# One batch's output tiles drained by ScalarE instead of VectorE, with x added between DRAM tensors, in a fused mixing and routed low-rank kernel

## The chip, the cores and the metric

One core of a Trainium2 chip runs the whole program. The metric is the device time of one execution in microseconds (us), as the median over several runs. All arithmetic is in 32-bit floats; the matrix products split each operand into a high and a low float32r part and use three products of the four.

## What is computed

Four batches of 1024 tokens with 1024 channels. Per channel and batch a bidirectional decaying sum over tokens mixes the side input f with itself, is gated by a sigmoid of x, and goes through a linear layer with a routed low-rank addition; the input x is added at the end.

```python
ek, ekv = exp(min(f, 30)), exp(min(f, 30)) * f
num = fwd_scan(ekv) + bwd_scan(ekv) - ekv + exp(min(u + f, 30)) * f      # state * decay + next
den = fwd_scan(ek)  + bwd_scan(ek)  - ek  + exp(min(u + f, 30))
y = sigmoid(x) * num / max(den, 1e-8) * (0.8 + 0.2 * tf)                 # 4 x 1024 x 1024
h = silu(y @ rw1.T + rb1)                                                # router, 64 wide
logits = h @ rw2.T + rb2 + gates                                         # 16 experts, top 2
coeff = softmax of the top two, 0 elsewhere
out = x + y @ W.T + bias + sum over experts of (coeff * (y @ A_e.T)) @ B_e.T
```

## The kernel before, in words

Everything lies channel-major: 128 channels on the partitions, tokens along the free dimension. A **unit** is one block of 128 channels of one batch with all 1024 tokens; there are 32, eight (CB) per batch. A **group** G is half the tokens (512) of one batch, so there are eight groups; groups 0 and 1 are the first batch. An output tile e = 8 G + j is 128 output channels j by 512 tokens.

Each engine has a program of its own, one loop over 41 **steps** s, and semaphores tie them. In step s:

- VectorE (loop at L856) runs for unit s the forward scans of the denominator (L704) and the numerator (L708), the `ratio` of unit s - 1 (L747), the backward scan of the denominator (L713), `p2` (L718), `sum_den` (L723), `scale_e` of unit s + 1 (L692) and the backward scan of the numerator (L734).
- ScalarE (L493) does `scale_end_den` (L414), `scale_end_num` (L414), `split_hi` (y_hi, L402), `exp_uk` (L391), `exp_k` (L385), `sigmoid_r` (L426), a table load (L478), and `inverse` (L430, L432), in that order.
- GpSimd (L638) does `sum_n` (L580) and `gate_n` (L586) of unit s - 1, `split_lo` (y_lo, L612), and `p1` of unit s + 1 (L602). The forward scan of step s + 1 waits for that p1.
- SyncE issues the loads of f (`load_k`, L294) and x (`load_r`, L299) for the next units, the weights, and the loads of x tiles for the output.

TensorE takes the finished y tiles: for a group `hid` (router), `low_rank`, `base` (the linear layer), `logits`, `spread` (routing weights onto partitions) and `expert`. Groups 0 and 1 get the lower half of the linear layer's sum as soon as half the channels are there: 16 part tiles, which ScalarE copies to the buffer `xo` (`drain_part`, L476) and SyncE stores into `out`. The upper half with the experts comes later. For these first 16 tiles VectorE runs `evacuate` (L754): PSUM tile plus bias plus an x tile that SyncE had loaded into the same `xo` buffer, written to `xo`; then GpSimd issues `add_out` (L636), a DMA that adds the tile onto what is stored in `out`. `xo` has six buffers (tile e uses e % 6). The units of the second batch are 8 to 15; group 2 is its late half of tokens, and TensorE takes unit 14, then 15, last. Unit 15 is handled in two halves (`HALVED`).

The order of the extra work of the first batch (steps CB to CB + 6, that is 8 to 14) is written out by hand in tables keyed by step and by place within the step: `hidden_at`, `silu_at`, `routing_at`, `weigh_at`, `evacs_at` for VectorE (places AFTER_FWD and so on, L163), `adds_at` for GpSimd (AFTER_GATE: after gate_n; AFTER_LO: after split_lo), `x_loads_at` for SyncE. The routing of group 1 lies in step CB + 4 = 12 after the forward scan of the denominator, its `weigh` (L818) after the ratio; the routing of group 0 lies in step 9 after the backward scan of the denominator, its weigh after p2. After routing, ScalarE makes wx_hi (L470) and GpSimd wx_lo (L625), both needed by `expert`; in steps 9 and 12 GpSimd does wx_lo ahead of p1.

From group 2 on (`SPLIT`) nothing is added by DMA: VectorE evacuates with bias and x, and SyncE stores. In the reader's listing:

Of the kernel before, what the change touches and what calls it, by code (L numbers as in the profile page):

```python
# [7 lines left out]
def decay_mix_with_routed_lora_channel_major(nc, x_cm, f_cm, cond, w, u, w_router_a, w_base, w_expert, bias, rb1, rw2,  # L8
# [25 lines left out]
    with ExitStack() as ctx:  # L34
# [6 lines left out]
        def sem(name):  # L41
            return ctx.enter_context(nc.semaphore(name))
# [117 lines left out]
        def base_from(G):  # L160
# [4 lines left out]
        silu_at = {(CB + 1, AFTER_FWD): 0, (CB + 3, AFTER_BWD_NUM): 1}  # L165
        routing_at = {(CB + 1, AFTER_BWD_DEN): 0, (CB + 4, AFTER_FWD): 1}
        weigh_at = {(CB + 1, AFTER_P2): 0, (CB + 4, AFTER_RATIO): 1}
        evacs_at = {(CB + 2, AFTER_FWD): (0, 1), (CB + 2, AFTER_FWD_NUM): (1, 2), (CB + 2, AFTER_RATIO): (2, 3),
                    (CB + 2, AFTER_SUM): (3, 5), (CB + 2, AFTER_BWD_NUM): (5, 6), (CB + 3, AFTER_FWD_NUM): (6, 7),
                    (CB + 3, AFTER_RATIO): (7, 8), (CB + 4, AFTER_BWD_NUM): (8, 10), (CB + 5, AFTER_FWD): (10, 11),  # L170
                    (CB + 5, AFTER_FWD_NUM): (11, 12), (CB + 5, AFTER_RATIO): (12, 13), (CB + 5, AFTER_SUM): (13, 14),
                    (CB + 5, AFTER_BWD_NUM): (14, 15), (CB + 6, AFTER_FWD): (15, 16)}
        AFTER_GATE, AFTER_LO = range(2)
        adds_at = {(CB + 2, AFTER_LO): (0, 3), (CB + 3, AFTER_GATE): (3, 6), (CB + 4, AFTER_GATE): (6, 8),
                   (CB + 5, AFTER_GATE): (8, 10), (CB + 5, AFTER_LO): (10, 13), (CB + 6, AFTER_GATE): (13, 16)}
        AFTER_K, AFTER_R = range(2)
        x_loads_at = {(CB, AFTER_R): (2, 6), (CB + 1, AFTER_R): (0, 2), (CB + 2, AFTER_R): (6, 9),
                      (CB + 3, AFTER_R): (9, 12), (CB + 4, AFTER_R): (12, 14), (CB + 5, AFTER_K): (14, 16),
                      (CB + 6, AFTER_K): (16, 19), (CB + 6, AFTER_R): (19, 20)}

        def tiles(table, s, place):
            return range(*table.get((s, place), (0, 0)))
# [13 lines left out]
        def held(g):  # L196
            return g >= 2 * CB and g % CB in (1, 5)

        def stores_to(slot, end):
            return sum(1 for e in range(PARTS, end) if e % XBUF == slot)  # L200
# [77 lines left out]
        def _(sp):  # L278
# [59 lines left out]
            for s in range(STEPS):  # L338
# [27 lines left out]
                for n in chunks_at(load_late_steps, s):  # L366
                    load_chunk(n)
                if s == CB:
                    for i in range(PBUF):
                        sp.wait_ge(part_stored[i], 16 * (PARTS // PBUF))  # L370
                if s == CB + 1:
                    sp.wait_ge(w_lo_ready, CHUNKS)
                for e in tiles(x_loads_at, s, AFTER_R):
                    load_x(e)
            for i in range(XBUF):
                sp.wait_ge(out_added[i], 16 * len(range(i, PARTS, XBUF)))
                sp.wait_ge(out_stored[i], 16 * stores_to(i, GROUPS * CB))

        @block.scalar
        def _(act):  # L380
# [91 lines left out]
            def drain_part(p):  # L472
# [20 lines left out]
            for s in range(STEPS):  # L493
# [7 lines left out]
                if s < UNITS:  # L501
                    if s == 0:
                        act.wait_ge(recip_ready, 1)
                    scale_end_den(s)
                if q == 1:
                    exp_gap(G)
                if s == CB + 1:
                    copy_xa(0)
                if s == CB + 4:
                    exp_gap(1)  # L510
                    copy_xa(1)
                if s < UNITS:
                    if s - 1 in HALVED:
                        split_late_hi(s - 1)
                    scale_end_num(s)
                if 0 < s <= UNITS and not late_split:
                    split_hi(s - 1)
                if q == 1:
                    split_wx(G)
                if s < UNITS:  # L520
                    exp_uk(s)
                if s == CB + 4:
                    split_wx(1)
                if s + 1 < UNITS:
                    exp_k(s + 1)
                if s == CB + 1:
                    exp_gap(0)
# [7 lines left out]
                if s < UNITS:  # L535
                    sigmoid_r(s)
                if z_of == 0:
                    low_rows(z_of)
                if z_of >= 0:
                    sigmoid_z(z_of)  # L540
                if s < UNITS or z_of >= 0:
                    exps()
                if s == CB + 1:
                    split_wx(0)
                if s < UNITS:
                    if s == 0:
                        act.wait_ge(gains_ready, 2)
                    inverse(s)
                for n in new:
                    weights_hi(n)  # L550
# [7 lines left out]
        def _(pool):  # L558
# [74 lines left out]
            def add_out(e):  # L633
                pool.wait_ge(evacuated, e + 1)
                pool.wait_ge(part_stored[e % PBUF], 16 * (e // PBUF + 1))
                nc.gpsimd.dma_start(at(out, e), xo[:, e % XBUF, :], accum_op=ALU.add).then_inc(out_added[e % XBUF], 16)  # L636

            for s in range(STEPS):  # L638
# [7 lines left out]
                if s - 1 in HALVED:  # L646
                    split_late_lo(s - 1)
                    split_lo(s - 1)
                for e in tiles(adds_at, s, AFTER_GATE):
                    add_out(e)  # L650
# [4 lines left out]
                if 0 < s <= UNITS and not late_split and s - 1 not in HALVED:  # L655
                    split_lo(s - 1)
                for e in tiles(adds_at, s, AFTER_LO):
                    add_out(e)
# [13 lines left out]
        def _(dve):  # L672
# [77 lines left out]
            def evacuate(G, j):  # L750
                e, bank = G * CB + j, out_bank(G, j)
                dve.wait_ge(out_done, e + 1)
                dve.wait_ge(x_in[e % XBUF], 16 * (e // XBUF + 1))
                nc.vector.scalar_tensor_tensor(out=xo[:, e % XBUF, :], in0=acc[:, bank, :], scalar=bias_sb[:, j:j + 1],  # L754
                                               in1=xo[:, e % XBUF, :], op0=ALU.add, op1=ALU.add).then_inc(evacuated, 1)
# [88 lines left out]
            def first_groups(s, place):  # L844
                if (s, place) in hidden_at:
                    hidden(hidden_at[s, place])
                if (s, place) in silu_at:
                    silu(silu_at[s, place])
                if (s, place) in routing_at:
                    routing(routing_at[s, place])  # L850
                if (s, place) in weigh_at:
                    weigh(weigh_at[s, place])
                for e in tiles(evacs_at, s, place):
                    evacuate(*divmod(e, CB))

# [288 lines left out]
```

## Time and profile before

| what | value |
|---|---|
| median of 3 runs | 688.63 us (688.4 to 689.16) |
| profiled execution, its own time | 688.6 us |
| its span in the profile | 686.6 us |
| TensorE busy | 598.7 us (87%) |
| VectorE busy | 526.6 us (77%) |
| GpSimd busy | 368.1 us (54%) |
| ScalarE busy | 357.1 us (52%) |
| DMA queue of SyncE | 73.79 MB |
| DMA queue of GpSimd | 4.20 MB |

The names in the profile: PE is TensorE (matmul), PEld its weight loads, DVE is VectorE, ACT is ScalarE, POOL is GpSimd, SPq is SyncE's DMA queue. A row names the line of the kernel, the tile written and the tiles read. In brackets at its end stands how long the engine was idle before it and whose work ended that. Times are in us from the start of the span unless ns is said. Busy shares over the whole span hide that the stages differ: VectorE is over 90% busy up to some 310 us, TensorE from some 260 us to the end.

### The profile page before, as it was taken

Reading aid. Unit: us, or ns where it says so; the run is one execution under the profiler, and the core shown is the slowest. Engines: PE = TensorE matmul, PEld = TensorE weight load, DVE = VectorE, ACT = ScalarE, POOL = GpSimd, SP = SyncE. Lnnn points to the kernel's source line nnn. Section 1 sums busy time; section 2 is a strip of 40 time slices with the busy share of each in tenths; the row PEclk is TensorE's granted clock in tenths of the full one; section 3 lists DMA queues with packets and bytes.
Section 4 is the critical chain, followed back from the end, with each engine's and each line's share of the span. In section 5 each row is a group of like instructions: output and inputs, shape, how many; then the busy total and the mean of one; then the engine's idle time right before and its main releaser. Section 6 shows DMA issues by size and latency. Waiting matters only on the chain.

```text
span 686.6 us, 7030 instructions
## 1 busy us (share of the span) xinstructions
PE 598.7 (87%) x2626; PEld 490.1 (71%) x2626; DVE 526.6 (77%) x573; ACT 357.1 (52%) x418; POOL 368.1 (54%) x183
## 2 busy tenths in 40 slices
PE   0153588989999937999999999999999999999997
PEld 0132466768878825887888878888888888888886
DVE  7999999999999999998899797979897532021202
ACT  4777789785656666655655554656465420011000
POOL 1789997867868876647544753565465501000100
PEclk9976799989999978999999999999999999999999
DMA  5323476522945831234423360427132402040022
GB/s 190 122 90 121 124 254 205 194 100 71 215 107 121 203 113 64 74 113 160 141 73 113 109 198 32 153 63 242 33 116 84 124 29 66 27 153 1 25 67 76
DMA packets 33169, 78.42 MB, mean 114 GB/s; under 512 B 4720, under 2 KB 4848, under 8 KB 33136
## 3 DMA queue, kind: packets, MB, share of 16 engines
q1 hardware_dynamic: 30832, 73.79, 33.2%
q0 software_dynamic: 2304, 4.20, 3.8%
q8 instruction: 20, 0.33, 0.2%
q14 instruction: 13, 0.11, 0.0%
HBM read 57.00 MB, written 20.97 MB: 114 GB/s over the span
## 4 chain that ended last, share of the span: by engine, by line
PE 49%; DVE 25%; POOL 16%; issue 7%; ACT 1%; DMA 1%; SPq 0%; DVEq 0%; POOLq 0%; ACTq 0%
PE acc L925 15%; PE acc L927 15%; PE acc L926 15%; DVE mix L713 5%; POOL mix L602 4%; POOL kv L580 4%; POOL yr L586 4%; DVE yr L747 3%; DVE mix L708 3%; DVE eu L723 3%; DVE kv L718 2%; DVE xo L754 2%; POOL y_lo L612 2%; DVE mix L734 2%; PE acc L936 1%
## 5 line engine op out<-in xcount | busy, mean ns | idle before, releaser
L925 PE MATMUL acc<-y_hi,wa_hi 128*128 128x512 f32 x640 | 258.5, 404 | 59.7 <-POOL y_lo L612 52.7
L926 PE MATMUL acc<-y_lo,wa_hi 128*128 128x512 f32 x640 | 255.3, 399 | 0.0
L927 PE MATMUL acc<-y_hi,wa_lo 128*128 128x512 f32 x640 | 254.8, 398 | 0.0
L925 PEld LDWEIGHTS acc<-y_hi,wa_hi 128*128 128x128 f32 x640 | 124.1, 194 | 89.3 <-POOL y_lo L612 54.1
L927 PEld LDWEIGHTS acc<-y_hi,wa_lo 128*128 128x128 f32 x640 | 123.8, 194 | 26.7
L926 PEld LDWEIGHTS acc<-y_lo,wa_hi 128*128 128x128 f32 x640 | 124.2, 194 | 25.6
L602 POOL TENSOR_TENSOR mix<-mix,kv 128x1024 f32<-128x1024 f32 x31 | 74.3, 2397 | 75.7 <-DVE mix L692 59.4
L754 DVE SCALAR_TENSOR_TENSOR xo<-acc,bias_sb,xo 128x512 f32<-128x512 f32 x64 | 46.4, 735 | 75.2 <-PE acc L927 75.2
L612 POOL TENSOR_TENSOR y_lo<-yr,y_hi 128x1024 fp32r<-128x1024 f32 x31 | 74.3, 2398 | 50.2 <-ACT y_hi L402 50.2
L625 POOL TENSOR_TENSOR wx_lo<-xa,wx_hi 128x512 fp32r<-128x512 f32 x16 | 20.9, 1329 | 129.3 <-ACT wx_hi L470 129.3
L580 POOL TENSOR_TENSOR kv<-mix,kv 128x1024 f32<-128x1024 f32 (+1 forms) x32 | 75.4, 2356 | 5.3 <-DVE mix L734 5.3
L704 DVE TENSOR_TENSOR_SCAN mix<-d_ps,mix 128x1024 f32<-128x1024 f32 x32 | 73.1, 2284 | 5.8 <-POOL mix L602 5.7
L414 ACT ACTIVATE mix<-mix,rdelta_g 128x1 f32<-128x1 f32 x64 | 18.6, 296 | 111.6 <-DVE mix L708 71.6
L586 POOL TENSOR_TENSOR yr<-kv,yr 128x1024 f32<-128x1024 f32 (+1 forms) x32 | 75.2, 2351 | 2.5
L713 DVE TENSOR_TENSOR_SCAN mix<-d_ps,mix 128x1023 f32<-128x1023 f32 x32 | 74.8, 2336 | 0.3 <-ACT mix L414 0.3
L734 DVE TENSOR_TENSOR_SCAN mix<-d_ps,mix 128x1023 f32<-128x1023 f32 (+1 forms) x32 | 73.7, 2303 | 0.0
L708 DVE TENSOR_TENSOR_SCAN mix<-d_ps,mix 128x1024 f32<-128x1024 f32 x32 | 72.7, 2272 | 0.0
L402 ACT ACTIVATE y_hi<-yr 128x1024 fp32r<-128x1024 f32 x31 | 32.9, 1060 | 51.6 <-DVE yr L747 51.6
L747 DVE SCALAR_TENSOR_TENSOR yr<-eu,limit_g,yr 128x1024 f32<-128x1024 f32 (+1 forms) x32 | 40.2, 1257 | 22.5 <-POOL yr L586 22.5
L925 PE MATMUL acc<-wx_hi,wb_hi 128*128 128x512 f32 x128 | 50.0, 391 | 1.8 <-POOL wx_lo L625 1.8
L926 PE MATMUL acc<-wx_lo,wb_hi 128*128 128x512 f32 x128 | 49.8, 389 | 0.0
L927 PE MATMUL acc<-wx_hi,wb_lo 128*128 128x512 f32 x128 | 49.8, 389 | 0.0
(98 smaller groups left out, 738.3 us busy)
## 6 DMA issues: line engine op xcount, KB each, us to landing
kv<-f_cm SPq DMA_DIRECT2D x32, 512.0 KB, 3.6
yr<-x_cm SPq DMA_DIRECT2D x32, 512.0 KB, 3.4
out<-xo SPq DMA_DIRECT2D x64, 256.0 KB, 4.2
xo<-x_cm SPq DMA_DIRECT2D x64, 256.0 KB, 3.9
out<-xo POOLq DMA_DIRECT2D x16, 256.0 KB, 6.8
xa<-w_base SPq DMA_DIRECT2D x5, 512.0 KB, 3.5
xo<-w_base SPq DMA_DIRECT2D x3, 512.0 KB, 5.7
xo<-w_router_a SPq DMA_DIRECT2D x2, 480.0 KB, 3.6
```

Of the source, the lines that this page charges most:

```text
L580: nc.gpsimd.tensor_tensor(kv[:, g % 2, t], num_of(g)[:, t], kv[:, g % 2, t], ALU.add).then_inc(n_ready, 1)
L586: nc.gpsimd.tensor_tensor(yr[:, g % 2, t], kv[:, g % 2, t], yr[:, g % 2, t], ALU.mult).then_inc(gated, 1)
L602: nc.gpsimd.tensor_tensor(num_of(g), den_of(g), kv[:, g % 2, :], ALU.mult).then_inc(p1_ready, 1)
L612: nc.gpsimd.tensor_tensor(slots(y_lo, g), yr[:, g % 2, :].rearrange("p (h t) -> p h t", h=2), slots(y_hi, g).bitcast(fp32), ALU.subtract). ...
L704: nc.vector.tensor_tensor_scan(den_of(g), decay(g, T), den_of(g), 0.0, ALU.mult, ALU.add).then_inc(den_fwd, 1)
L708: nc.vector.tensor_tensor_scan(num_of(g), decay(g, T), num_of(g), 0.0, ALU.mult, ALU.add).then_inc(num_fwd, 1)
L713: nc.vector.tensor_tensor_scan(rev(den_of(g)), decay(g, T - 1), rev(den_of(g)), den_of(g)[:, T - 1:T], ALU.mult, ALU.add).then_inc(den_bwd, 1)
L734: nc.vector.tensor_tensor_scan(a[:, stop - 1::-1], decay(g, stop), a[:, stop - 1::-1], a[:, stop:stop + 1], ALU.mult, ALU.add).then_inc(nu ...
L747: nc.vector.scalar_tensor_tensor(out=yr[:, g % 2, t], in0=eu[:, t], scalar=limit_f[:, g:g + 1], in1=yr[:, g % 2, t], op0=ALU.min, op1=ALU. ...
L925: nc.tensor.matmul(out_ap, wh, yh, start=start, stop=False)
L926: nc.tensor.matmul(out_ap, wh, yl, start=False, stop=False)
L927: return nc.tensor.matmul(out_ap, wl, yh, start=False, stop=stop)
```

## The change

The 16 output tiles of groups 0 and 1 are no longer evacuated by VectorE. ScalarE does it (`drain`: activation Identity with the bias), in places of its own program set by a new table, `drains_at`. x isn't loaded for them any more; GpSimd issues eight DMAs (`add_x`) that add a whole unit of x (128 rows of 1024 floats, both token halves) from DRAM onto `out` in DRAM, after the part tiles are stored there, and `add_out` of a tile waits for the x add of its channels. A drain of tile e from the seventh on waits until the output add of tile e - 6 has landed, because it writes the same `xo` buffer. The routing of group 1 moves within step 12 from after the forward scan to after the backward scan of the denominator, and its weigh from after the ratio to after sum_den. On ScalarE the copy of xa and the exponential of the gap for group 1 move behind exp_uk, and the split of wx behind the table load. Of SyncE's x loads, those for tiles 0 to 15 go, and 16 to 19 move.

```diff
-        routing_at = {(CB + 1, AFTER_BWD_DEN): 0, (CB + 4, AFTER_FWD): 1}
-        weigh_at = {(CB + 1, AFTER_P2): 0, (CB + 4, AFTER_RATIO): 1}
-        evacs_at = {(CB + 2, AFTER_FWD): (0, 1), (CB + 2, AFTER_FWD_NUM): (1, 2), (CB + 2, AFTER_RATIO): (2, 3),
-                    (CB + 2, AFTER_SUM): (3, 5), (CB + 2, AFTER_BWD_NUM): (5, 6), (CB + 3, AFTER_FWD_NUM): (6, 7),
-                    (CB + 3, AFTER_RATIO): (7, 8), (CB + 4, AFTER_BWD_NUM): (8, 10), (CB + 5, AFTER_FWD): (10, 11),
-                    (CB + 5, AFTER_FWD_NUM): (11, 12), (CB + 5, AFTER_RATIO): (12, 13), (CB + 5, AFTER_SUM): (13, 14),
-                    (CB + 5, AFTER_BWD_NUM): (14, 15), (CB + 6, AFTER_FWD): (15, 16)}
+        routing_at = {(CB + 1, AFTER_BWD_DEN): 0, (CB + 4, AFTER_BWD_DEN): 1}
+        weigh_at = {(CB + 1, AFTER_P2): 0, (CB + 4, AFTER_SUM): 1}
+        AFTER_END_DEN, AFTER_END_NUM, AFTER_EXP_UK, AFTER_EXP_K, AFTER_SIGMOID, AFTER_INVERSE = range(6)
+        drains_at = {(CB + 1, AFTER_INVERSE): (0, 1), (CB + 2, AFTER_END_DEN): (1, 3), (CB + 2, AFTER_EXP_UK): (3, 4),
+                     (CB + 2, AFTER_SIGMOID): (4, 5), (CB + 2, AFTER_INVERSE): (5, 6), (CB + 3, AFTER_END_DEN): (6, 7),
+                     (CB + 3, AFTER_EXP_UK): (7, 8), (CB + 4, AFTER_INVERSE): (8, 9), (CB + 5, AFTER_END_DEN): (9, 11),
+                     (CB + 5, AFTER_EXP_UK): (11, 12), (CB + 5, AFTER_SIGMOID): (12, 13),
+                     (CB + 5, AFTER_INVERSE): (13, 14), (CB + 6, AFTER_END_DEN): (14, 15),
+                     (CB + 6, AFTER_EXP_UK): (15, 16)}
         AFTER_GATE, AFTER_LO = range(2)
-        adds_at = {(CB + 2, AFTER_LO): (0, 3), (CB + 3, AFTER_GATE): (3, 6), (CB + 4, AFTER_GATE): (6, 8),
-                   (CB + 5, AFTER_GATE): (8, 10), (CB + 5, AFTER_LO): (10, 13), (CB + 6, AFTER_GATE): (13, 16)}
+        x_adds_at = {(CB, AFTER_LO): (0, 1), (CB + 1, AFTER_GATE): (1, 3), (CB + 1, AFTER_LO): (3, 4),
+                     (CB + 2, AFTER_GATE): (4, 8)}
+        adds_at = {(CB + 2, AFTER_LO): (0, 2), (CB + 3, AFTER_GATE): (2, 5), (CB + 3, AFTER_LO): (5, 7),
+                   (CB + 4, AFTER_GATE): (7, 8), (CB + 5, AFTER_LO): (8, 11), (CB + 6, AFTER_GATE): (11, 13),
+                   (CB + 6, AFTER_LO): (13, 15), (CB + 7, AFTER_GATE): (15, 16)}
-        x_loads_at = {(CB, AFTER_R): (2, 6), (CB + 1, AFTER_R): (0, 2), (CB + 2, AFTER_R): (6, 9),
-                      (CB + 3, AFTER_R): (9, 12), (CB + 4, AFTER_R): (12, 14), (CB + 5, AFTER_K): (14, 16),
-                      (CB + 6, AFTER_K): (16, 19), (CB + 6, AFTER_R): (19, 20)}
+        x_loads_at = {(CB + 6, AFTER_R): (16, 18), (CB + 7, AFTER_R): (18, 20)}
...
+            def drain(e):
+                G, j = divmod(e, CB)
+                act.wait_ge(out_done, e + 1)
+                if e < 2:
+                    act.wait_ge(w_lo_ready, CHUNKS)
+                elif e < XBUF:
+                    act.wait_ge(part_stored[(e - 2) % PBUF], 16 * (PARTS // PBUF))
+                else:
+                    act.wait_ge(out_added[e % XBUF], 16 * (e // XBUF))
+                nc.scalar.activation(xo[:, e % XBUF, :], acc[:, out_bank(G, j), :], ACT.Identity,
+                                     bias=bias_sb[:, j:j + 1]).then_inc(evacuated, 1)
...
+                drains(s, AFTER_END_DEN)
                 if q == 1:
                     exp_gap(G)
                 if s == CB + 1:
                     copy_xa(0)
-                if s == CB + 4:
-                    exp_gap(1)
-                    copy_xa(1)
...
                     exp_uk(s)
+                drains(s, AFTER_EXP_UK)
                 if s == CB + 4:
-                    split_wx(1)
+                    copy_xa(1)
+                    exp_gap(1)
...
-                if s == CB + 1:
-                    split_wx(0)
+                if s in (CB + 1, CB + 4):
+                    split_wx((s - CB) // 4)
...
             def add_out(e):
                 pool.wait_ge(evacuated, e + 1)
-                pool.wait_ge(part_stored[e % PBUF], 16 * (e // PBUF + 1))
+                pool.wait_ge(x_added[e % CB], 16)
                 nc.gpsimd.dma_start(at(out, e), xo[:, e % XBUF, :], accum_op=ALU.add).then_inc(out_added[e % XBUF], 16)
+
+            def add_x(j):
+                pool.wait_ge(part_stored[j % PBUF], 16 * ((j + CB) // PBUF + 1))
+                nc.gpsimd.dma_start(out[j], x_cm[j], accum_op=ALU.add, max_dma_last_dim=4 * T).then_inc(x_added[j], 16)
...
-                for e in tiles(evacs_at, s, place):
-                    evacuate(*divmod(e, CB))
```

The other drains stand after `scale_end_num`, `exp_k`, `sigmoid_r` and `inverse` (places without an entry in the table do nothing).

## Rows read from the trace of the kernel before

**Rows 1.** Waits, TensorE, 150 to 400 us: who waited, for whom, us, times, longest.
```profile
PE acc L936 <- POOL y_lo L612: 8.9, 1, 8.9
PE acc L936 <- POOL y_lo L619: 5.4, 1, 5.4
```

**Rows 2.** Busy time by stretch; at the end granted clock, DMA share, GB/s.
```profile
240.00:260.00 20.00, 6.25 (x17) 4.12 (x15) 19.00 (x14) 12.28 (x15) 15.49 (x10) 0.71 0.30 101
```

**Rows 3.** Timeline of VectorE, the forward scans that open steps 9 to 15.
```profile
136.41 2.27 DVE L704 TENSOR_TENSOR_SCAN mix<-d_ps,mix 128x1024 f32<-128x1024 f32 x1
...
157.09 2.29 DVE L704 TENSOR_TENSOR_SCAN mix<-d_ps,mix 128x1024 f32<-128x1024 f32 x1 [1.27 <-POOL mix L602]
...
174.01 2.27 DVE L704 TENSOR_TENSOR_SCAN mix<-d_ps,mix 128x1024 f32<-128x1024 f32 x1
...
189.54 2.27 DVE L704 TENSOR_TENSOR_SCAN mix<-d_ps,mix 128x1024 f32<-128x1024 f32 x1
...
210.20 2.27 DVE L704 TENSOR_TENSOR_SCAN mix<-d_ps,mix 128x1024 f32<-128x1024 f32 x1
...
226.45 2.27 DVE L704 TENSOR_TENSOR_SCAN mix<-d_ps,mix 128x1024 f32<-128x1024 f32 x1
...
240.42 2.29 DVE L704 TENSOR_TENSOR_SCAN mix<-d_ps,mix 128x1024 f32<-128x1024 f32 x1 [0.26 <-POOL mix L602]
```

**Rows 4.** The chain of waits around step 15: start, us, what.
```profile
237.98 2.24 POOL mix L602
240.33 2.38 POOL kv L580
242.78 2.35 POOL yr L586
245.23 1.28 DVE yr L747
...
251.76 1.17 POOL mix L602
```

**Rows 5.** Groups of instructions, VectorE, 156 to 232 us.
```profile
L754 DVE SCALAR_TENSOR_TENSOR xo<-acc,bias_sb,xo 128x512 f32<-128x512 f32 x16 | 11.5, 728 | 0.0
```

**Rows 6.** Timeline of GpSimd in step 10.
```profile
159.49 2.40 POOL L586 TENSOR_TENSOR yr<-kv,yr 128x1024 f32<-128x1024 f32 x1
165.23 2.42 POOL L612 TENSOR_TENSOR y_lo<-yr,y_hi 128x1024 fp32r<-128x1024 f32 x1 [3.34 <-ACT y_hi L402]
167.58 2.80 POOL L636 DMA_DIRECT2D out<-xo  x3
171.28 2.40 POOL L602 TENSOR_TENSOR mix<-mix,kv 128x1024 f32<-128x1024 f32 x1 [0.90 <-DVE mix L692]
```

**Rows 7.** Groups of instructions, ScalarE, 100 to 260 us.
```profile
L391 ACT ACTIVATE eu<-kv,u_g 128x1024 f32<-128x1024 f32 x10 | 11.0, 1102 | 0.0
...
L402 ACT ACTIVATE y_hi<-yr 128x1024 fp32r<-128x1024 f32 x10 | 10.6, 1061 | 11.3 <-DVE yr L747 11.3
...
L476 ACT COPY xo<-acc 128x512 f32<-128x512 f32 x9 | 4.7, 583 | 0.0
```

**Rows 8.** Timeline of SyncE's queue, x loads behind the first output adds.
```profile
173.83 0.33 SPq L312 DMA_DIRECT2D xo<-x_cm  x1
...
176.41 0.33 SPq L312 DMA_DIRECT2D xo<-x_cm  x1
```

**Rows 9.** DMA queues, whole span: packets, MB, share of 16 engines.
```profile
q1 hardware_dynamic: 30832, 73.79, 33.2%
q0 software_dynamic: 2304, 4.20, 3.8%
```

**Rows 10.** Timeline of VectorE, the first weighing of step 9.
```profile
150.18 0.69 DVE L818 TENSOR_TENSOR xa<-acc,xa 128x512 f32<-128x512 f32 x1
```

**Rows 11.** Timeline of TensorE, behind a wait for the router.
```profile
139.41 1.86 PE L974 MATMUL acc<-rw_sb,fan 64*128 64x16 f32 x8 [2.45 <-DVE fan L764]
...
141.78 0.63 PE L926 MATMUL acc<-y_lo,wa_hi 128*128 128x512 f32 x1
```

More of the change, by code:

```diff
@@ L197, in held, with x_loads_to @@
             return g >= 2 * CB and g % CB in (1, 5)
+        def x_loads_to(e):
+            return sum(1 for i in range(PARTS, e + 1) if i % XBUF == e % XBUF)
         def stores_to(slot, end):
@@ L213, in decay_mix_with_routed_lora_channel_major @@
         part_out = sem("part_out")
+        x_added = [sem(f"x_added{j}") for j in range(CB)]
         out_added = [sem(f"out_added{i}") for i in range(XBUF)]
@@ L367, in _ @@
                     load_chunk(n)
-                if s == CB:
-                    for i in range(PBUF):
-                        sp.wait_ge(part_stored[i], 16 * (PARTS // PBUF))
-                if s == CB + 1:
-                    sp.wait_ge(w_lo_ready, CHUNKS)
                 for e in tiles(x_loads_at, s, AFTER_R):
                     load_x(e)
+            for j in range(CB):
+                sp.wait_ge(x_added[j], 16)
             for i in range(XBUF):
@@ L476, in drain_part, with drains @@
                 nc.scalar.copy(xo[:, 2 + p % PBUF, :], acc[:, p % 5, :]).then_inc(part_out, 1)
+            def drain(e):
[9 more added lines that the diff above has]
+                                     bias=bias_sb[:, j:j + 1]).then_inc(evacuated, 1)
+            def drains(s, place):
+                for e in tiles(drains_at, s, place):
+                    drain(e)
             exps = lambda: nc.scalar.preload_act_table_set("natural_log_exp_and_others")
@@ L515, in _ @@
                     scale_end_num(s)
+                drains(s, AFTER_END_NUM)
                 if 0 < s <= UNITS and not late_split:
@@ L521, in _ @@
                     exp_uk(s)
+                drains(s, AFTER_EXP_UK)
                 if s == CB + 4:
-                    split_wx(1)
+                    copy_xa(1)
+                    exp_gap(1)
                 if s + 1 < UNITS:
                     exp_k(s + 1)
+                drains(s, AFTER_EXP_K)
                 if s == CB + 1:
@@ L536, in _ @@
                     sigmoid_r(s)
+                drains(s, AFTER_SIGMOID)
                 if z_of == 0:
@@ L542, in _ @@
                     exps()
-                if s == CB + 1:
-                    split_wx(0)
+                if s in (CB + 1, CB + 4):
+                    split_wx((s - CB) // 4)
                 if s < UNITS:
@@ L548, in _ @@
                     inverse(s)
+                drains(s, AFTER_INVERSE)
                 for n in new:
@@ L648, in _ @@
                     split_lo(s - 1)
+                for j in tiles(x_adds_at, s, AFTER_GATE):
+                    add_x(j)
                 for e in tiles(adds_at, s, AFTER_GATE):
@@ L656, in _ @@
                     split_lo(s - 1)
+                for j in tiles(x_adds_at, s, AFTER_LO):
+                    add_x(j)
                 for e in tiles(adds_at, s, AFTER_LO):
@@ L752, in evacuate @@
                 dve.wait_ge(out_done, e + 1)
-                dve.wait_ge(x_in[e % XBUF], 16 * (e // XBUF + 1))
+                dve.wait_ge(x_in[e % XBUF], 16 * x_loads_to(e))
                 nc.vector.scalar_tensor_tensor(out=xo[:, e % XBUF, :], in0=acc[:, bank, :], scalar=bias_sb[:, j:j + 1],
```

## The prediction

> **What bounds the kernel now.** I first read who waited for whom on TensorE. From 150 us on it has two long waits, 8.9 us and 5.4 us, both for a y_lo tile of GpSimd [rows 1]. The stretch 240 to 260 us is the only later one with a hole: TensorE is busy 6.25 of 20 us there, at a granted clock of 0.71 [rows 2]. Both waits are for the last two channel tiles (units 14 and 15) of the second batch; the late half of unit 15 lets TensorE go at 260.55. Behind that TensorE is all but full to the end. So the question is one number: how much earlier does unit 15 come? A microsecond won there is a microsecond of the kernel; one won anywhere else is nothing.
>
> What sets unit 15 is the loop of steps on VectorE. Its step starts are the forward scans [rows 3]: steps 9 to 15 start at 136.41, 157.09, 174.01, 189.54, 210.20, 226.45 and 240.42. They took 20.7, 16.9, 15.5, 20.7, 16.25 and 14.0 us (9 to 14). The chain of waits shows a step without extras as a cycle through two engines: p1, sum_n and gate_n on GpSimd, then the ratio and three more passes on VectorE, and p1 again [rows 4], 251.76 - 237.98 = 13.8 us. No step falls below 13.8 us by taking evacuations from VectorE alone.
>
> **What is removed.** 16 evacuations, 11.5 us of VectorE, 0.728 each [rows 5]. They start some 0.65 us apart from their neighbours, so they are worth at most 16 x 0.65 = 10.4 us, by steps 6, 2, 2, 5 and 1 of them (10 to 14). Against the floor of the cycle much of it is not to be had. The 16 x loads leave SyncE's queue; nothing that decides waits for them, so I cost that at nothing.
>
> **What is added.** On GpSimd, eight more DMA issues. Three in a row took 2.80 us there, 0.93 each [rows 6]. A DRAM to DRAM issue has no row; between nothing and twice 0.93, I take 0.93, since it moves the same number of 128 rows. On ScalarE 16 drains; the nearest row is the copy of the same shape, 0.583 [rows 7]. I take 0.6. On the DMA queue of GpSimd, 8 accumulations of 512 KB.
>
> **Step 10.** gate_n ends where its row does, 161.9 [rows 6]. Then come four x adds (to 165.6), y_lo 2.4 (168.0), two output adds (169.9), p1 2.4 (172.3). VectorE without its evacuations would be ready at 170.7, so GpSimd decides: step 11 starts at 172.4 instead of 174.0, a gain of 1.6. Drains 1 to 5 fall into idle time of ScalarE.
>
> **Step 11, the place that decides.** The drain of tile 6 stands after scale_end_den, ahead of scale_end_num, split_hi and exp_uk, and it waits until the output add of tile 0 has landed, because both use buffer 0. Before, only an x load on SyncE waited for that. When does add 0 land? GpSimd issues it at 168.0, behind x adds 4 to 7 in the same queue. Three output adds issued from 167.58 released the x loads that waited for them at 173.83 and 176.41, the third one between [rows 6, 8]: 6.2 us to the first, then 1.3 us for each further 256 KB. The queue's row says 3.8% of the span for 16 adds, 1.63 us each, and 6.2 us per MB against 3.1 for plain transfers [rows 9]. Thus 2.6 to 3.3 us per x add. The first, issued at 161.9, lands at 169.4 to 169.8, the fourth at 177.2 to 179.7, add 0 1.3 to 1.6 later, 178.5 to 181.3. I take 180.0. From there: drain 0.6 (180.6), scale_end_num 0.3, y_hi 1.06 and exp_uk 1.10 [rows 7] (183.0, as they overlap a little), on VectorE p2, sum_den, hidden, scale_e, backward_num and silu, 6.5 together: step 12 starts at 189.5, where it did before (189.54). Without that wait p2 would start at 180.7 and step 12 at 187.2. So 2.3 us of gain are given back.
>
> **Step 12**, with the routing moved. Its form is now that of step 9, where the first weighing starts at 150.18, 13.8 after the step's start, and the next step 6.9 after it [rows 3, 10]. Step 12 has no silu (-0.6) and weighs one pass later (+1.13): 13.8 - 0.6 + 1.1 + 6.9 = 21.2 us against 20.7. The cause of the tail is that p1 stands behind both wx_lo on GpSimd. Loss 0.5.
>
> **Steps 13 and 14.** Step 13: three output adds (2.8) stand between y_lo and p1 and push p1 by 1.1 beyond the cycle: 14.85 against 16.25, gain 1.4. Step 14: 13.9 against 14.0, gain 0.1. Step 15 has one add in a gap of 2.5 us: nothing.
>
> **Sum.** 1.6 - 1.6 (the gain of step 10 and its loss again at the start of step 12) - 0.5 + 1.4 + 0.1 = 1.0 us. The profiled execution took 688.6 (span 686.6 and 2.0 around it), the median of the runs shown is 688.63, so the sum may be held against either: 688.6 - 1.0 = **687.6 us**.
>
> **TensorE's own work.** With the routing about 6 us later it waits some 4 us for the fan tiles, and after a wait of 2.45 us its matmuls took 0.63 instead of 0.39 us for about 5 us [rows 11]; with that, group 1 ends about 5 us later. The cover is the 8.9 us wait [rows 1], so it costs nothing. If that cover went, each further microsecond would count; also, drains 8 and 14 stand ahead of scale_end on ScalarE and would hold VectorE once TensorE is about 1 to 2 us later still.
>
> **A rule of the skill.** The trace has 6.2 to 6.9 us from issue to landing for an accumulating DMA of 256 KB, 1.3 of it its own share of the queue [rows 6, 8]. The Trainium skill, "DMA: Bandwidth & Descriptors", section "Anatomy of one DMA", gives about 2.0 us plus bytes over 436 KB per us, which would make 3.2 us of an x add, 1.2 of it transfer; an estimate by that page has the queue all but empty when add 0 is issued. By that rule the wait in step 11 is gone. The trace speaks against its rate for accumulation, but not about DRAM as the source.
>
> **Rivals.**
> 1. *The queue is empty in time.* If an x add takes 2.3 us or less, add 0 lands before 177.6 (161.9 + 4.9 + 4 x 2.3 + 1.3 = 177.3), no wait arises, step 12 starts at 187.2 and the gain is 1.6 + 0.7 - 0.5 + 1.4 + 0.1 = 3.3: 685.3 us. For it: 1.3 us per 256 KB holds a part that need not double. Against: the queue row's 6.2 us per MB. Chance 0.25, all of it faster.
> 2. *The queue is deeper, slower.* The source and the destination are both DRAM, and loads of f and x run beside it. One mechanism: the drain of tile 6 waiting for add 0. Every microsecond beyond 180.0 is lost in full, and from 181.0 on the kernel is slower than before. At 4 us per x add, add 0 lands at about 184.5: 4.5 lost, 688.6 + 3.5 = 692.1. Nearest row: plain transfers are half as dear [rows 9], none is this dear. Chance 0.20.
> 3. *TensorE gets late by the later routing* and ScalarE's drains stall VectorE behind it: 1 to 2 us of loss on top of the forecast's gain, 689.5. For it: the wait and the low clock above; against: margins worked out as 1 to 2 us. Chance 0.09.
> 4. *Issuing a DRAM to DRAM add costs GpSimd far less* than 0.93 and the queue is empty too: step 11 starts at 170.7 and the gain nears 5: 683.6. Chance 0.06.
>
> **How the numbers follow.** The forecast has 0.40; its own range is 685.6 to 689.4, from add 0 at 178.5 to 181.3 (gains of 2.5 and -0.3) with half a microsecond either way. What a measurement can tell from no change is 0.2%, 1.4 us. It is passed on the fast side if add 0 lands before 179.6, which I give 0.15 of the forecast's 0.40, and 0.03 lies beyond it on the slow side. Faster: 0.15 + 0.25 + 0.06 = 0.46. Same: 0.22. Slower: 0.03 + 0.20 + 0.09 = 0.32. The range leaves out rival 4 and the deep end of rival 2: 684.6 to 692.2.
>
> **What the profile after would show.** Right: on ScalarE the drain of tile 6 ends at about 180.6 with an idle time of 5 us ahead, put down to a DMA or to nothing; VectorE idle about 2 us before p2 of step 11; steps 10 to 14 of 15.3, 17.1, 21.2, 14.85 and 13.9 us; TensorE's first wait shrunk from 8.9 to under 4 us, a new one ahead of the fan spreading, and unit 15 some 1.0 us earlier, at 259.5. Wrong: no idle time ahead of drain 6 (then rival 1), or GpSimd's four x adds taking other than 3.7 us, or step 12 far from 21.2.

## The result, and the profile after

The changed kernel takes 692.45 us (median of 6 runs, 691.9 to 693.85) against 689.01 for the kernel before (6 runs): ratio 1.0053, 95% interval 1.0042 to 1.0064. It is slower by 3.4 us by the medians and 3.6 by the ratio. The forecast was 687.6 with a range up to 692.2; the size was that of the second rival, but, as the rows show, not its mechanism. The profiled execution of the changed kernel took 693.85 us (span 692.1), 1.4 above its median.

Waits of TensorE from 150 to 400 us, changed kernel (who waited, for whom, us, times, longest):

```profile
PE acc L966 <- POOL y_lo L643: 6.1, 1, 6.1
PE acc L1011 <- DVE fan L842: 5.4, 1, 5.4
PE acc L1004 <- DVE fan L796: 4.0, 2, 2.1
PE acc L966 <- POOL y_lo L636: 3.8, 1, 3.8
```

The long wait for unit 14 went from 8.9 [rows 1] to 3.8 us, the one for the late half of unit 15 grew from 5.4 to 6.1, and others came: 5.4 us for the fan tiles of the later routing, and 4.0 in two places for the router. (One more wait for fan tiles, 2.6 us, ends at 149.5, just ahead of this stretch.) The two waits for units 14 and 15, changed kernel:

```profile
254.80 0.50 PE L966 MATMUL acc<-y_hi,wr 128*128 128x512 f32 x1 [3.83 <-POOL y_lo L636]
...
265.23 0.80 PE L966 MATMUL acc<-y_hi,wr 128*128 128x512 f32 x1 [6.06 <-POOL y_lo L643]
```

The last of them lets TensorE go at 265.23, against 260.55 before and 259.5 in the forecast. The forward scans that open steps 9 to 15 on VectorE, changed kernel:

```profile
137.24 2.27 DVE L736 TENSOR_TENSOR_SCAN mix<-d_ps,mix 128x1024 f32<-128x1024 f32 x1
...
158.94 2.29 DVE L736 TENSOR_TENSOR_SCAN mix<-d_ps,mix 128x1024 f32<-128x1024 f32 x1 [0.27 <-POOL mix L626]
...
178.62 2.29 DVE L736 TENSOR_TENSOR_SCAN mix<-d_ps,mix 128x1024 f32<-128x1024 f32 x1 [6.06 <-POOL mix L626]
...
194.55 2.29 DVE L736 TENSOR_TENSOR_SCAN mix<-d_ps,mix 128x1024 f32<-128x1024 f32 x1
...
216.20 2.29 DVE L736 TENSOR_TENSOR_SCAN mix<-d_ps,mix 128x1024 f32<-128x1024 f32 x1 [1.30 <-POOL mix L626]
...
231.05 2.29 DVE L736 TENSOR_TENSOR_SCAN mix<-d_ps,mix 128x1024 f32<-128x1024 f32 x1 [1.24 <-POOL mix L626]
...
245.04 2.29 DVE L736 TENSOR_TENSOR_SCAN mix<-d_ps,mix 128x1024 f32<-128x1024 f32 x1 [0.37 <-POOL mix L626]
```

The scan that opens step 11 stood idle for 6.06 us waiting for GpSimd's p1. Step 10 took 178.62 - 158.94 = 19.7 us instead of the forecast's 15.3. Held against the starts of before [rows 3], the rest is close to the forecast: step 12 took 21.65 (forecast 21.2), step 13 14.85 (14.85), step 14 13.99 (13.9). GpSimd in step 10, changed kernel (idle time before an instruction in brackets):

```profile
163.69 2.52 POOL L664 DMA_DIRECT2D out<-x_cm  x3
170.31 0.84 POOL L664 DMA_DIRECT2D out<-x_cm  x1 [4.11 <-issue]
170.87 2.71 POOL L636 TENSOR_TENSOR y_lo<-yr,y_hi 128x1024 fp32r<-128x1024 f32 x1
173.23 1.23 POOL L660 DMA_DIRECT2D out<-xo  x1
175.29 0.86 POOL L660 DMA_DIRECT2D out<-xo  x1 [0.84 <-issue]
175.87 2.72 POOL L626 TENSOR_TENSOR mix<-mix,kv 128x1024 f32<-128x1024 f32 x1
```

Three x adds are issued in 2.52 us, 0.84 each. The fourth stands for 4.11 us, and "issue" says that it waits for nothing that the profile shows as a semaphore. It goes out 6.6 us after the first of the four was begun, and 0.3 us after that first one had landed (6.3 us from issue to landing, so at 170.0). The same shows once more at the second output add (0.84) and in step 11 (1.49). y_lo, the output adds and p1 stand behind it. In the kernel before, such a pause is nowhere: its bursts of three go through in 2.80 us [rows 6], and no fourth one is ever in flight. ScalarE's drain of tile 6, the place that the forecast feared:

```profile
181.59 0.69 ACT L491 ACTIVATE xo<-acc,bias_sb 128x512 f32<-128x512 f32 x1 [0.35 <-DMA out<-xo]
```

It waited 0.35 us, because the step itself had come 6 us late. The stretch that answers to the one of before [rows 2] is fuller, 15.35 us of TensorE instead of 6.25: the wait for unit 14 has shrunk, and the one for unit 15 now lies mostly behind 260 us (259.2 to 265.2). Then the two queues, whole span [rows 9]:

```profile
240.00:260.00 20.00, 15.35 (x60) 11.75 (x58) 19.18 (x14) 15.71 (x16) 16.47 (x10) 0.91 0.78 188
```

```profile
q1 hardware_dynamic: 28528, 69.59, 31.2%
q0 software_dynamic: 3456, 8.39, 6.7%
```

### The profile page after: what moved, and what is told of

Read it like the earlier page. It is cut to its first block, busy times and chain, and to the rows that moved or that the text cites. A ratio compares the mean times of both kernels' runs of the same rounds, so it can differ in the third digit from the quotient of the medians.

```text
span 692.1 us, 7024 instructions
## 1 busy us (share of the span) xinstructions
PE 599.1 (87%) x2626; PEld 491.7 (71%) x2626; DVE 518.5 (75%) x557; ACT 367.2 (53%) x434; POOL 374.5 (54%) x191
## 3 DMA queue, kind: packets, MB, share of 16 engines
q0 software_dynamic: 3456, 8.39, 6.7%
## 4 chain that ended last, share of the span: by engine, by line
PE 52%; POOL 21%; DVE 18%; issue 8%; ACT 1%; DMA 0%; POOLq 0%; DVEq 0%; SPq 0%; ACTq 0%
PE acc L955 16%; PE acc L956 15%; PE acc L957 15%; POOL kv L604 5%; POOL mix L626 5%; POOL yr L610 5%; DVE mix L745 4%; DVE yr L779 3%; POOL y_lo L636 2%; PE acc L1011 2%; DVE kv L750 2%; DVE eu L755 2%; DVE mix L740 2%; POOL out L660 1%; PE acc L966 1%
## 5 line engine op out<-in xcount | busy, mean ns | idle before, releaser
L626 POOL TENSOR_TENSOR mix<-mix,kv 128x1024 f32<-128x1024 f32 x31 | 75.8, 2446 | 70.3 <-DVE mix L724 53.0
L786 DVE SCALAR_TENSOR_TENSOR xo<-acc,bias_sb,xo 128x512 f32<-128x512 f32 x48 | 35.0, 739 | 75.2 <-PE acc L957 75.2
L604 POOL TENSOR_TENSOR kv<-mix,kv 128x1024 f32<-128x1024 f32 (+1 forms) x32 | 76.9, 2405 | 5.3 <-DVE mix L766 5.3
```

Of the source, the lines that this page charges most:

```text
L604: nc.gpsimd.tensor_tensor(kv[:, g % 2, t], num_of(g)[:, t], kv[:, g % 2, t], ALU.add).then_inc(n_ready, 1)
L626: nc.gpsimd.tensor_tensor(num_of(g), den_of(g), kv[:, g % 2, :], ALU.mult).then_inc(p1_ready, 1)
```

## The experiments

A descriptor is the entry that tells a DMA engine one piece to move. **Theory A**, formed after the result: GpSimd's DMAs need room for their descriptors, and the 1024 bytes per partition that the kernel gives (`dynamic_dma_scratch_size`) hold three DMAs of 128 rows and not four; the fourth stands on GpSimd until one has landed. The eight x adds bring 8 x 144 = 1152 packets, 9 per DMA engine and add, as the count 3456 - 2304 [rows 9] says, the same as an output add. **Theory B**: the transfers are what lasts, with or without room. A third question was the price of the later routing. A fourth, whether the semaphore that an x add waits for came late, is answered by run 1 too, which leaves every wait as it is. Step lengths, from the scans' starts, in us; times are medians, and the kernel before is measured anew with each set (688.6 to 689.0):

| kernel | 10 | 11 | 12 | 13 | 14 | time |
|---|---|---|---|---|---|---|
| before | 16.9 | 15.5 | 20.7 | 16.25 | 14.0 | 689.0 |
| forecast | 15.3 | 17.1 | 21.2 | 14.85 | 13.9 | 687.6 |
| changed | 19.7 | 15.9 | 21.65 | 14.85 | 14.0 | 692.45 |
| 1 more room | 14.85 | 16.3 | 21.3 | 14.9 | 14.0 | 687.46 |
| 2 fewer descriptors | 14.8 | 16.4 | 21.6 | 14.9 | 14.0 | 687.38 |
| 3 x adds spread | 14.8 | 15.75 | 21.6 | 14.9 | 14.0 | 686.96 |
| 4 routing back | 19.8 | 15.85 | 19.8 | 14.9 | 13.95 | 689.51 |
| 5 before, routing later | 16.9 | 15.5 | 22.9 | 16.25 | 14.0 | 693.32 |
| 6 remedies 1 to 3 | 14.0 | 14.9 | 21.35 | 14.85 | 13.9 | 685.54 |
| 7 as 6, routing and adds moved | 14.0 | 14.8 | 22.1 | 13.9 | 13.9 | 685.24 |
| 8 no x adds | 14.1 | 15.7 | 21.6 | 14.8 | 14.1 | 686.32 |
| 9 as 7, routing after the ratio | 14.0 | 14.8 | 20.1 | 13.9 | 13.9 | 682.85 |
| 10 as 6, routing back | 14.0 | 14.8 | 23.35 | 14.9 | 13.9 | 687.18 |

That the start of step 15 decides is borne out: in the profiled executions of all eleven kernels, held against the one before, that start and the time moved together to within 1.0 us (run 9: 6.3 us earlier and 5.6 faster; run 1: 1.9 earlier and 1.0 faster).

### 1. More room

```diff
-    nc = bacc.Bacc("TRN2", target_bir_lowering=False, num_devices=1, dynamic_dma_scratch_size=1024)
+    nc = bacc.Bacc("TRN2", target_bir_lowering=False, num_devices=1, dynamic_dma_scratch_size=1472)
```

> The changed kernel with 1472 instead of 1024 bytes per partition for the descriptors of GpSimd's DMAs, nothing else. Theory A (GpSimd stands still at the fourth x add because the room for descriptors holds only three of its DMAs): the 4.1 us idle ahead of the fourth x add goes, step 10 falls from 19.7 to about 15.4 us; the wait then shows up as ScalarE's drain of tile 6 waiting 3 to 5 us for the output add of tile 0, step 11 grows from 15.9 to about 17 to 18, and the time is 689 us, give or take 1. Theory B (the wait is for the transfers themselves, whatever room there is): the idle time stays 4 us and the time 692.4.

Measured: 687.46 us, ratio to before 0.9977 (0.9967 to 0.9986). This one number turns a loss of 3.4 to 3.6 us into a gain of 1.4 to 1.6, somewhat more than the expectation had (688 to 690). GpSimd and then ScalarE, in this kernel:

```profile
161.96 3.38 POOL L664 DMA_DIRECT2D out<-x_cm  x4
```

```profile
179.03 0.69 ACT L491 ACTIVATE xo<-acc,bias_sb 128x512 f32<-128x512 f32 x1 [4.36 <-DMA out<-xo]
```

The four x adds go out without a pause, 0.845 us each. The drain of tile 6 now does what the forecast said: it waits 4.36 us for the output add of tile 0, which landed at 179.0 (forecast 180.0). Step 11 opens at 172.06 (forecast 172.4) and step 12 at 188.33 (189.5). Theory A stands; theory B is out, since the transfers were the same. One more pause may be hidden here: the two output adds behind the four x adds took 2.65 us instead of 1.80 in run 6. The profile counts that as the first one's duration (1.76 us) and not as idle time, but the second started at 168.45, 0.26 us after the first x add had landed.

### 2. Fewer descriptors

```diff
-                nc.gpsimd.dma_start(out[j], x_cm[j], accum_op=ALU.add, max_dma_last_dim=4 * T).then_inc(x_added[j], 16)
+                nc.gpsimd.dma_start(out[j], x_cm[j], accum_op=ALU.add, max_dma_last_dim=8 * T).then_inc(x_added[j], 16)
```

> The changed kernel with the x adds' descriptors allowed 8 KB instead of 4 KB, so half as many. Theory A: what is limited is the number of descriptors, an x add takes 5 instead of 9 per DMA engine, four of them fit beside an output add, the 4.1 us wait goes and the time is 688.5 to 689.5. Rival A2 (what is limited is the number of DMAs in flight, three): the wait stays, 692.4. If the descriptors are not merged, the packet count of GpSimd's queue stays 3456 and nothing changes.

Measured: 687.38 us, ratio 0.9973 (0.9962 to 0.9985), a microsecond under what was expected. The queue's row and GpSimd's output adds:

```profile
q0 software_dynamic: 2944, 8.39, 6.7%
```

```profile
161.90 3.22 POOL L664 DMA_DIRECT2D out<-x_cm  x4
166.88 2.65 POOL L660 DMA_DIRECT2D out<-xo  x2
176.73 0.87 POOL L660 DMA_DIRECT2D out<-xo  x1
179.29 0.88 POOL L660 DMA_DIRECT2D out<-xo  x1 [1.69 <-issue]
180.44 0.87 POOL L660 DMA_DIRECT2D out<-xo  x1 [0.28 <-issue]
```

The bytes are the same, the packets 512 fewer (5 per DMA engine and x add instead of 9), and four x adds fit, with the first output add as a fifth in flight. So what fills up is descriptors and not the count of DMAs (rival A2). The output adds still have 128 rows each and stall at the fourth in flight (1.69 us). An estimate by the Trainium skill, "DMA: Bandwidth & Descriptors", sections "Terms" and "The descriptor swizzle": a descriptor has 16 bytes, and each DMA engine gets one for reading and one for writing per piece, so an add of 9 packets per engine would take 9 x 2 x 16 = 288 bytes. By that, three take 864 and four 1152 bytes, five 1440, and four halved x adds with one output add 4 x 160 + 288 = 928: that agrees with the pauses above, but not with one issue of this run. The second output add started at 168.55 with three x adds and one output add in flight, 3 x 160 + 2 x 288 = 1056 bytes by that estimate, 32 more than the room. The traces alone give bounds: with 1024 bytes, 33 packets per DMA engine were in flight at once and 36 never were, so a packet takes 28.4 to 31.0 bytes (1024 / 36 and 1024 / 33), if a DMA holds its room until it has landed. For that it speaks that in the changed kernel and runs 2, 3, 4 and 8 each pause put to an issue ended 0.26 to 0.34 us after an earlier DMA had landed. How the room is counted exactly, and that reading and writing share it, is not shown.

### 3. The x adds spread

```diff
-        x_adds_at = {(CB, AFTER_LO): (0, 1), (CB + 1, AFTER_GATE): (1, 3), (CB + 1, AFTER_LO): (3, 4),
-                     (CB + 2, AFTER_GATE): (4, 8)}
+        x_adds_at = {(CB, AFTER_GATE): (0, 2), (CB, AFTER_LO): (2, 3), (CB + 1, AFTER_GATE): (3, 5),
+                     (CB + 1, AFTER_LO): (5, 6), (CB + 2, AFTER_GATE): (6, 8)}
```

> The changed kernel with the x adds issued earlier and never more than three in flight: two after gate_n and one after split_lo in step 8, two and one in step 9, two in step 10. Theory A: no wait of GpSimd in step 10, step 10 takes 14.0 us and step 11 15.4 with a wait of about 1 us at the output adds 5 and 6, no wait at the drain of tile 6; with steps 12 to 14 as measured (21.6, 14.9, 14.0) the time is 685 to 687 us, faster than the kernel before. Rival B (the accumulating traffic and the eight further issues cost it wherever they stand): 689 or more.

Measured: 686.96 us, ratio 0.9975 (0.9962 to 0.9988), within the expected 685 to 687. Step 10 fell to 14.8 and not to 14.0: the second output add is the fourth in flight again and stood 0.86 us, until 0.3 us after the first x add of that step had landed (the profile puts this idle time down to VectorE). In step 11 the pauses came where they were expected:

```profile
183.79 0.98 POOL L660 DMA_DIRECT2D out<-xo  x1 [1.29 <-issue]
185.07 0.86 POOL L660 DMA_DIRECT2D out<-xo  x1 [0.30 <-issue]
```

### 4. The routing back in its place

The edit undoes the routing's part of the change, in the tables of VectorE and in ScalarE's order:

```diff
-        routing_at = {(CB + 1, AFTER_BWD_DEN): 0, (CB + 4, AFTER_BWD_DEN): 1}
-        weigh_at = {(CB + 1, AFTER_P2): 0, (CB + 4, AFTER_SUM): 1}
+        routing_at = {(CB + 1, AFTER_BWD_DEN): 0, (CB + 4, AFTER_FWD): 1}
+        weigh_at = {(CB + 1, AFTER_P2): 0, (CB + 4, AFTER_RATIO): 1}
```

> The changed kernel with the routing of group 1 and its weighing back in their places of before (after the forward scan and after the ratio of step 12), ScalarE's order too. Theory A: the later place costs by itself, step 12 falls from 21.7 to 19 to 19.5 us, TensorE gets the fan tiles without its 5.4 us wait, and the time falls by 2 to 2.5 us to 690.2. Rival: the place is neutral since the step's work on VectorE is the same, and the time stays within 0.7 us of 692.4.

Measured: 689.51 us, ratio 1.0009 (0.9999 to 1.0019), not to be told from the kernel before: 2.9 us less than the changed kernel, somewhat more than expected. VectorE's scans open step 12 at 193.37 and step 13 at 213.16:

```profile
193.37 2.29 DVE L738 TENSOR_TENSOR_SCAN mix<-d_ps,mix 128x1024 f32<-128x1024 f32 x1 [0.33 <-POOL mix L628]
...
213.16 2.29 DVE L738 TENSOR_TENSOR_SCAN mix<-d_ps,mix 128x1024 f32<-128x1024 f32 x1 [0.26 <-POOL mix L628]
```

Of the 2.9 us step 12 explains 1.9 (21.65 to 19.8). In the two profiled executions, which are 3.1 us apart, the other 1.2 us lie ahead of step 10, where both kernels run the same program; so they tell nothing of the routing, and why the medians differ by more than 1.9 is open.

### 5. The later routing alone, in the kernel before

The same lines as in the change (routing, weigh, ScalarE's order), nothing else.

> The kernel before with nothing but the routing of group 1 and its weighing in their later places in step 12 and ScalarE's order for it. Theory A: the later place has a price of its own, about what its undoing gave (step 12 fell from 21.7 to 19.8 us): step 12 grows from 20.7 to about 22.5 us (the two evacuations at its end then lie inside the wait for p1, so perhaps 21.5), the time is 689.8 to 691, slower by 1 to 2 us. Rival: neutral, 688.9 give or take 0.7.

Measured: 693.32 us (691.2 to 695.2 in 4 runs), ratio 1.0075 (1.0053 to 1.0098), a loss of 4.6 us and more than expected. The profiled execution, at 691.23 the fastest, shows 22.9 us for step 12. VectorE at its end:

```profile
211.06 0.75 DVE L752 SCALAR_TENSOR_TENSOR xo<-acc,bias_sb,xo 128x512 f32<-128x512 f32 x1 [2.07 <-PE acc L925]
212.42 0.75 DVE L752 SCALAR_TENSOR_TENSOR xo<-acc,bias_sb,xo 128x512 f32<-128x512 f32 x1 [0.61 <-PE acc L925]
213.09 2.28 DVE L702 TENSOR_TENSOR_SCAN mix<-d_ps,mix 128x1024 f32<-128x1024 f32 x1
```

My expectation had the evacuations inside the wait for p1. Instead, TensorE got the fan tiles late (a wait of 3.5 us for them), its first output tiles came late, and VectorE, which still evacuates here, waited 2.07 and 0.61 us for them. Step 12 grew by 2.2 us (20.7 to 22.9); why the other runs of this kernel are 1 to 4 us slower than the profiled one is open.

### 6. The three remedies together

> The changed kernel with all three remedies for GpSimd's DMA queue at once: 1472 bytes of room, 8 KB descriptors, and the x adds spread over steps 8 to 10. Theory A: no idle time put to the issue of a DMA in steps 10 and 11, the drain of tile 6 does not wait; step 10 about 14.2, step 11 about 15.2, step 12 starts at 186.6 to 187.2 instead of 188.4, and the time is 685.5 to 686.5, a microsecond under each remedy alone. Rival (they remove the same wait and what is left is GpSimd's own issue time): no better than 687.

Measured: 685.54 us, ratio 0.9952 (0.9936 to 0.9969). In steps 10 and 11 GpSimd has no idle time put to an issue. The drain of tile 6 waits 0.16 us. Steps 10 and 11 are at 14.0 and 14.9 us, the first near the cycle's floor of 13.8.

### 7. Routing and output adds moved again

On top of 6, the routing after the numerator's forward scan, the weighing after the backward scan, ScalarE's order of before, and the output adds at most two after gate_n and one after split_lo (in step 10 two after split_lo):

```diff
-        routing_at = {(CB + 1, AFTER_BWD_DEN): 0, (CB + 4, AFTER_BWD_DEN): 1}
-        weigh_at = {(CB + 1, AFTER_P2): 0, (CB + 4, AFTER_SUM): 1}
+        routing_at = {(CB + 1, AFTER_BWD_DEN): 0, (CB + 4, AFTER_FWD_NUM): 1}
+        weigh_at = {(CB + 1, AFTER_P2): 0, (CB + 4, AFTER_BWD_DEN): 1}
...
+        adds_at = {(CB + 2, AFTER_LO): (0, 2), (CB + 3, AFTER_GATE): (2, 4), (CB + 3, AFTER_LO): (4, 5),
+                   (CB + 4, AFTER_GATE): (5, 7), (CB + 4, AFTER_LO): (7, 8), (CB + 5, AFTER_GATE): (8, 10),
+                   (CB + 5, AFTER_LO): (10, 11), (CB + 6, AFTER_GATE): (11, 13), (CB + 6, AFTER_LO): (13, 14),
+                   (CB + 7, AFTER_GATE): (14, 16)}
```

> As the run before, with the routing of group 1 after the forward scan of the numerator in step 12 and its weighing after the backward scan of the denominator, ScalarE's order of before for it, and GpSimd's output adds at most two after gate_n and one after split_lo. Theory A: steps 10 to 14 take 14.2, 15.1, 18.9, 13.9 and 13.8 us, step 15 starts 6 to 7.4 us earlier than before, and the time is 681.5 to 683. Rival (TensorE's own work becomes the bound, as its 8.9 us wait ahead of unit 14 is used up): 684 to 686.

Measured: 685.24 us, ratio 0.9950 (0.9933 to 0.9966), no faster than run 6 and a miss by 2 to 4 us. The time is the one that the rival had named (684 to 686), but not for its reason: TensorE still waits 5.5 us ahead of unit 14 and 5.4 ahead of the late half of unit 15. Step 13 fell from 14.85 to 13.9, as expected of moving two adds out of the gap ahead of p1. Step 12 took 22.1 and not 18.9. The routing's first instruction on VectorE and TensorE's logits:

```profile
194.03 0.23 DVE L810 TENSOR_TENSOR lg<-acc,rbg 128x64 f32<-128x64 f32 x1 [2.07 <-PE acc L1007]
```

```profile
192.93 1.06 PE L1007 MATMUL acc<-rw_sb,fan 64*128 64x16 f32 x8
```

VectorE stood 2.07 us for logits that TensorE had not made yet. I had set the routing by VectorE's time alone. The remaining 1.1 us of the miss in step 12 are not accounted for.

### 8. No x adds

x is missing from the first batch's output in this kernel. SyncE's waits for the x adds at the end go as well.

```diff
-        x_adds_at = {(CB, AFTER_LO): (0, 1), (CB + 1, AFTER_GATE): (1, 3), (CB + 1, AFTER_LO): (3, 4),
-                     (CB + 2, AFTER_GATE): (4, 8)}
+        x_adds_at = {}
...
-                pool.wait_ge(x_added[e % CB], 16)
+                pool.wait_ge(part_stored[e % PBUF], 16 * (e // PBUF + 1))
```

> The changed kernel without the eight x adds, so that x is missing from the first batch's output; an output add then waits for its part tile's store alone, as before. Theory A (the x adds' place and room in the queue cost all that was lost): step 10 takes 14.0 to 14.5 us instead of 19.7, the drain of tile 6 waits less than 0.5 us, the time is 685 to 686.5. Rival (ScalarE's drains themselves or the later routing outweigh the evacuations): 688.5 or more.

Measured: 686.32 us, ratio 0.9964 (0.9952 to 0.9976). Without them the changed kernel would gain 2.4 to 2.5 us. With room for them (1 and 2) they cost only 1.1. The output adds alone still stall at the fourth in flight, 1.28 us in step 11:

```profile
182.40 0.99 POOL L657 DMA_DIRECT2D out<-xo  x1 [1.28 <-issue]
```

### 9. The routing after the ratio

On top of 7: routing at `(CB + 4, AFTER_RATIO)`; ScalarE's `exp_gap(1)` and `copy_xa(1)` right behind `split_hi`, its `split_wx(1)` behind `exp_k`.

> As the version before it (all remedies, output adds at most two in a place), with the routing of group 1 after the ratio of step 12, ScalarE's gap exponential and copy of xa right behind split_hi, and its split of wx behind exp_k. Theory A (in the version before, VectorE stood 1.9 us ahead of the routing because TensorE's logits came only at 193.8): that wait falls under 0.6 us, step 12 falls from 22.1 to 19.5 to 20 us, and the time from 685.2 to 683, give or take 0.5. Rival (TensorE is the bound by now): its waits for y_lo of units 14 and 15 are gone and the time stays at 685.

Measured: 682.85 us, ratio 0.9913 (0.9896 to 0.9929), 5.8 us faster than before and the fastest of all. The routing's first instruction and the scan that opens step 13, which step 12 opened at 186.28:

```profile
192.77 0.22 DVE L810 TENSOR_TENSOR lg<-acc,rbg 128x64 f32<-128x64 f32 x1 [0.53 <-PE acc L1007]
...
206.39 2.29 DVE L739 TENSOR_TENSOR_SCAN mix<-d_ps,mix 128x1024 f32<-128x1024 f32 x1 [0.26 <-POOL mix L629]
```

### 10. All remedies, the routing back in its place of before

On top of 6, the edit of 4.

> The version with all three remedies for GpSimd's queue (685.5 us), with the routing back in its place of before, after the forward scan of step 12. Theory A (the worth of the place hangs on when TensorE's logits come): step 12 now starts at 186.3, the logits at about 191.5 to 192.5, so VectorE waits 3 to 4 us for them and step 12 takes 21.5 to 22.5 us, no shorter than the 21.4 of the later place: 685.5 to 686.5. Rival (the earlier place is the better one by itself, as undoing it in the changed kernel suggested): step 12 takes under 20 us and the time is 684 or less.

Measured: 687.18 us, ratio 0.9976 (0.9965 to 0.9987), slower than 6 by 1.6 and 0.7 above the expected range. The routing's first instruction:

```profile
192.79 0.23 DVE L809 TENSOR_TENSOR lg<-acc,rbg 128x64 f32<-128x64 f32 x1 [4.20 <-PE acc L1006]
```

The place that was worth 1.9 us in step 12 of run 4, where step 12 began at 193.4, costs 2.0 here, where it begins at 186.3. In run 4 TensorE waited for VectorE's router tile and made the logits by 194.6:

```profile
193.10 1.48 PE L1006 MATMUL acc<-rw_sb,fan 64*128 64x16 f32 x8 [1.74 <-DVE fan L798]
```

VectorE came to them only at 195.6 and had no wait. Here TensorE starts them at 191.7 without a wait of its own, so its own work sets them, and VectorE stands ready 4.2 us too early.

## Why the prediction was wrong

The step that failed is step 10, in the sentence that the four x adds run to 165.6: an overlap was taken for granted, that GpSimd can issue a fourth DMA while three are in flight. The issue time was well sized (0.84 measured, 0.93 taken). What was missing is that an issue can stand still: the fourth in flight waited 4.1 us and one output add 0.8 more. The forecast's 15.3 us became 19.7, from 1.6 us of gain to 2.8 of loss. The row that should have made me careful was there: nowhere in the kernel before are more than three of GpSimd's DMAs in flight [rows 6], so its trace could not show what the fourth does. I bounded the cost of an issue by twice a row and not by the time of a landing, 6.2 us [rows 6, 8], which was the honest upper end for a queue whose depth no row showed. Run 1, which changes nothing but the room, takes back the whole loss.

- **Step 11 and the drain of tile 6.** In the changed kernel the wait was 0.35 us and not 5, because GpSimd's stall had taken its place; step 11 took 15.9 (17.1). With the room enlarged the forecast mechanism appeared at its place, 4.4 us, with the add landing at 179.0 against 180.0, and the time was 687.46 against 687.6. So the forecast describes the kernel of run 1 in its mechanism. That the times agree to 0.1 us is partly luck: steps 10 and 11 were 0.45 and 0.8 us shorter than forecast, and step 15 opened 1.9 us earlier than before and not 1.0.
- **Step 12.** 21.65 against 21.2: right in size. My loss of 0.5 us against before was held to a step with two evacuations in it, and so hid the price of the move. Run 4 shows that the later place cost 1.9 us in that step, in a kernel where the change without it comes out even; it is the second term that I had too small. Run 10 shows why that is no general price.
- **Steps 13 and 14.** Right to 0.1 us.
- **TensorE.** The wait for the fan tiles came (5.4 us, 4 in the forecast), and the 8.9 us wait covered it, shrunk to 3.8. In the profiled execution step 9 also took 1.0 us more than before (21.7 against 20.7). The later of its two weighings waited 1.0 us for TensorE there: the spreading of the routing weights took 3.60 us instead of 1.95, at a granted clock of 0.69 from 150 to 155 us against 1.00 in the kernel before, and TensorE had stood idle for 2.57 us ahead of it. Run 1 has the same program up to there and shows 20.7, and the profiled execution is 1.4 us above its median, so I do not count this as an effect of the change.
- **Rival 2** named the time (692.1) for the wrong reason: a queue 4 us slow per x add. The rates were as forecast: in the changed kernel the x adds of step 10 landed 2.5 to 2.8 us apart, in run 1 2.5 to 3.5. Rival 1 would have had no wait at the drain once there was room; run 1 has one of 4.4 us. That goes against the rate of the Trainium skill, "DMA: Bandwidth & Descriptors", section "Anatomy of one DMA", too, by which the queue would have been all but empty. Of rival 3 one half came about: the later routing has a price (runs 4 and 5). The other, VectorE stalled behind ScalarE's drains, did not, since steps 13 and 14 took what was forecast. Rival 4 did not come about.
- **The sum.** Step 10 -2.8, step 11 -0.4, step 12 -1.0, step 13 +1.4, step 14 0, and -1.0 in step 9 of the profiled execution: 3.8 us later at the opening of step 15, with 0.8 more from before step 9. The scan there was at 240.42 before and is at 245.04 now, 4.6 us.

## What to carry to other kernels

Before adding DMAs to a queue whose descriptors a program writes, count how many are in flight at the worst place, times their descriptors, and hold that against the room; if no row of the trace has that many, bound the cost by a full landing, not by an issue. Work moved from one engine to others helps only down to the cycle that ties them (here 13.8 us), and each thing inserted has to fit the gap in that cycle where it stands. The best place for a consumer is when its producer is done: after any gain upstream, look again at what it waits for.

## What the hardware showed that I had not expected

- In this case GpSimd stands still, with all its later work, when it issues a fourth accumulating DMA of 9 packets per DMA engine with three in flight and 1024 bytes of room: 4.11 us, shown as idle time put to "issue". 1472 bytes took four x adds without a pause, and so did 1024 bytes with about half as many descriptors (5 instead of 9 per DMA engine). With 1024 bytes 33 packets per DMA engine were in flight at once (run 2), never 36; with 1472 bytes 45 were (run 1).
- Accumulating 512 KB from DRAM onto DRAM is no dearer to issue than 256 KB from the on-chip buffer (0.84 us against 0.93) and landed after a median of 7.2 us against 6.4.
